# Grouped attention: one reciprocal for two units' row sums, and GpSimd scales both units' probabilities behind it

## What is computed

```
x = x + _layernorm(_L0_attn_ref(_layernorm(x)))
x = x + _layernorm(_L0_ffn_ref(_layernorm(x), factors, bias))
x = x + _layernorm(_L1_attn_ref(_layernorm(x), norm_scale, split_scale, Wq, Wk, Wv, Wo))
x = x + _layernorm(_L1_ffn_ref(_layernorm(x), gate_w, up_w, down_w, gate_s, up_s, down_s))
```

```
q = (h @ Wq.T).reshape(b, s, H, dh)      # H = 8 heads of dh = 64
k = (h @ Wk.T).reshape(b, s, G, dh)      # G = 2 groups, as v
scores = jnp.einsum('bghsd,bgtd->bghst', q, k) / np.float32(np.sqrt(dh))
attn = jax.nn.softmax(scores, axis=-1)
out = jnp.einsum('bghst,bgtd->bghsd', attn, v)
return x + out @ Wo.T
```

## Time and profile before

| | us |
|---|---|
| median of 3 runs | 1664.28 (1664.16 to 1665.33) |
| span of the profiled execution | 1664.7 |
| PE busy | 1499.3 (90%) |
| PEld busy | 1215.0 (73%) |
| DVE busy | 1049.3 (63%) |
| ACT busy | 789.7 (47%) |
| POOL busy | 733.6 (44%) |
| mean granted TensorE clock | 0.967 |

### The profile page before, as it was taken

How to read it: one execution, slowest core, us unless ns; L and a number is a source line. 1 busy time by engine, 2 the same in 40 slices (tenths; PEclk the granted TensorE clock), 3 DMA queues, 4 the chain that set the end, 5 groups by cost and what they waited for, 6 DMA issues and landing times.

```text
span 1664.7 us, 23612 instructions
## 1 busy us (share of the span) xinstructions
PE 1499.3 (90%) x7332; PEld 1215.0 (73%) x7332; DVE 1049.3 (63%) x2091; ACT 789.7 (47%) x1506; POOL 733.6 (44%) x914
## 2 busy tenths in 40 slices
PE   4999987986899998999899998679899999999996
PEld 3778766865678786878687876457688888888885
DVE  5688847875888887888788877545424234234233
ACT  2334335645877877787778776322212222222131
POOL 3476742653444544454445445313233333333331
PEclk9999997997999999999999999889999999999998
DMA  4122002232000202020202020232110110100100
GB/s 151 54 99 74 27 1 70 78 124 102 1 1 1 77 1 78 1 77 1 78 1 77 1 95 1 76 101 76 45 51 1 51 39 12 50 26 25 50 26 26
DMA packets 41814, 80.17 MB, mean 48 GB/s; under 512 B 2416, under 2 KB 3440, under 8 KB 41712
## 3 DMA queue, kind: packets, MB, share of 16 engines
q1 hardware_dynamic: 41712, 78.93, 14.0%
HBM read 53.75 MB, written 25.17 MB: 47 GB/s over the span
## 4 chain that ended last, share of the span: by engine, by line
PE 57%; DVE 9%; issue 4%; POOL 3%; ACT 3%; DMA 1%; POOLq 0%; DVEq 0%; SPq 0%; ACTq 0%
PE f_inner L57 22%; PE g_side L1375 12%; PE f_down L1786 9%; PE g_score L57 5%; PE g_turned L1395 5%; DVE g_ptl L1299 2%; PE g_output L1421 2%; PE g_output L1423 2%; DVE g_neg_max L1285 1%; DVE f_wl L1710 1%; PE f_inner L1758 1%; POOL g_power L984 1%; ACT g_pth L1161 1%; DVE g_q L1214 1%; DVE f_hidden L1679 1%
## 5 line engine op out<-in xcount | busy, mean ns | idle before, releaser
L1010 POOL TENSOR_SCALAR g_prob<-g_prob,g_inv_sum 128x512 f32<-128x512 f32 x256 | 178.7, 698 | 321.6 <-DVE g_inv_sum L1290 321.4
L57 PE MATMUL f_inner<-f_xth,f_wh 128*128 128x512 f32 x704 | 282.2, 401 | 16.2 <-DVE f_wl L1710 12.9
L57 PE MATMUL f_inner<-f_xtl,f_wh 128*128 128x512 f32 x704 | 280.7, 399 | 0.0
L1679 DVE SCALAR_TENSOR_TENSOR f_hidden<-f_inner,f_inner_scale,f_silu 128x512 f32<-128x512 f32 x88 | 66.0, 750 | 315.5 <-PE f_inner L57 315.5
L1568 POOL TENSOR_TENSOR f_hl<-f_hidden,f_hh 128x512 fp32r<-128x512 f32 x88 | 128.1, 1456 | 298.7 <-DVE f_hh L1685 298.7
L1620 ACT ACTIVATE f_silu<-f_inner,f_inner_scale 128x512 f32<-128x512 f32 x88 | 60.7, 690 | 415.8 <-PE f_inner L57 415.8
L1285 DVE TENSOR_REDUCE g_neg_max<-g_score 128x1 f32<-128x512 f32 x256 | 175.2, 685 | 94.9 <-PE g_score L57 93.8
L1119 ACT ACTIVATE g_prob<-g_score,g_neg_max 128x512 f32<-128x512 f32 x256 | 177.1, 692 | 96.5 <-DVE g_neg_max L1285 94.2
L1395 PE MATMUL g_turned<-identity,g_prob 128*128 128x128 f32 x1024 | 156.3, 275 | 37.2 <-DVE g_ptl L1299 24.6
L1299 DVE TENSOR_TENSOR g_ptl<-g_turned,g_pth 128x512 fp32r<-128x512 f32 x256 | 173.6, 678 | 16.4 <-ACT g_pth L1161 14.7
L1161 ACT CAST g_pth<-g_turned 128x512 fp32r<-128x512 f32 x256 | 149.5, 584 | 59.4 <-PE g_turned L1395 57.6
(11 more groups left out here) (200 smaller groups left out, 3456.8 us busy)
## 6 DMA issues: line engine op xcount, KB each, us to landing
x_resident<-x SPq DMA_DIRECT2D x8, 1024.0 KB, 7.3
x_mixed<-x_resident SPq DMA_DIRECT2D x8, 1024.0 KB, 4.3
x_pair<-x_mixed SPq DMA_DIRECT2D x8, 1024.0 KB, 7.5
g_res<-x_mixed SPq DMA_DIRECT2D x8, 1024.0 KB, 6.9
x_attended<-g_res SPq DMA_DIRECT2D x8, 1024.0 KB, 5.1
x_pair<-x_attended SPq DMA_DIRECT2D x8, 1024.0 KB, 5.5
factor<-factors SPq DMA_DIRECT2D x7, 1024.0 KB, 5.4
out<-x_pair SPq DMA_DIRECT2D x7, 1024.0 KB, 4.3
```

The costliest lines, as they stand in the source:

```text
L57: last = nc.tensor.matmul(out, lhsT, rhs, start=(n == 0), stop=(n == len(pairs) - 1))
L1010: nc.gpsimd.tensor_scalar(prob[:, at, :], prob[:, at, :], inv_sum[:, at:at + 1], 1.0, ALU.mult, ALU.mult).then_inc(prob_ready, 1)
```

## The change

The reciprocal is taken at even steps alone, of two neighbouring columns of `row_sum`, for units u-2 and u-1. POOL scales both units behind it at the even step, and nothing at the odd one. At an odd step the rest of POOL's and DVE's step stands where it did.

```diff
-            def normalise(g, u):
-                wait_alone(pool, s, inv_ready, g + 1)
-                at = u % 4
-                nc.gpsimd.tensor_scalar(prob[:, at, :], prob[:, at, :], inv_sum[:, at:at + 1],
-                                        1.0, ALU.mult, ALU.mult).then_inc(prob_ready, 1)
+            def normalise_pair(b, u):
+                wait_alone(pool, s, inv_ready, b * (UNITS // 2) + u // 2)
+                for at in ((u + 2) % 4, (u + 3) % 4):
+                    nc.gpsimd.tensor_scalar(prob[:, at, :], prob[:, at, :], inv_sum[:, at:at + 1],
+                                            1.0, ALU.mult, ALU.mult).then_inc(prob_ready, 1)
...
-                if u > 0 or not first:
+                if u % 2 == 0 and (u > 0 or not first):
                     if not drain or u == 0:
-                        normalise(b * UNITS + u - 1, u + 3)
+                        normalise_pair(b, u)
...
-                if (u > 0 or not first) and (not drain or u == 0):
-                    at = (u - 1) % 4
+                if u % 2 == 0 and (u > 0 or not first) and (not drain or u == 0):
+                    at = (u + 2) % 4
                     dve.wait_ge(exp_ready, g)
-                    nc.vector.reciprocal(inv_sum[:, at:at + 1], row_sum[:, at:at + 1]).then_inc(inv_ready, 1)
+                    nc.vector.reciprocal(inv_sum[:, at:at + 2], row_sum[:, at:at + 2]).then_inc(inv_ready, 1)
```

## The result

| | before | with the change |
|---|---|---|
| median, 5 runs each | 1665.33 us (1664.16 to 1666.41) | 1674.16 us (1670.60 to 1675.44) |
| ratio | | 1.0049, 95% interval 1.0035 to 1.0062 |
| span of the profiled execution | 1664.7 us | 1673.6 us |
| mean granted TensorE clock | 0.967 | 0.959 |

The change makes the kernel slower by 0.49%, some 8 us (the medians lie 8.8 us apart); 6.2 us (0.37%) had been forecast. The 1674.16 us stand just above the range's end of 1673.8; but the range was built on a median of 1664.28 before, and 1.0049 times that is 1672.4, inside it.

A forecast was written before the change was run, and what follows sets the result against it. It took TensorE (PE), busy 90% of the span, as the bound. 6 x (0.50 + 0.57 - 0.07) = 6.0, -0.2 for batch 0 and +0.4 for batch 7 gave +6.2 us: 1670.5 us (+0.37%), range 1665.2 to 1673.8.

The forecast's parts named there:

- PE's path: Steps 3 to 10: POOL's second scales part holds up ScalarE, then DVE, then PE's transposes; its delay forecast +0.50 us.
- Pair at step 4: POOL's second part of the next batch's scales starts behind two scalings, at 490.28 instead of 489.78: +0.50 us.
- Even unit: Unit 6's scaling now follows step 8's reciprocal, so PE's step 10 transposes come 1.17 behind it, not 0.86: +0.31 us.
- `g_ol` behind the pair: Step 8: POOL's `g_ol` queues behind two scalings, delaying PE's first output projection of step 10: +0.57 us, not given back.
- Odd reciprocals: Step 15's removed reciprocal shortens a gapless DVE row for which PE waits: -0.07 us; other odd steps then wait for PE.
- Batch 0: DVE-bound in steps 5 to 21: -0.07 in some six odd steps, +0.24 in one even step, -0.2 us.
- Batch 7: Same `g_ol` delay (+0.5), pairs +0.2 once or twice, odd steps 0.07 back three or four times: +0.4 us.
- Sum of the waits: Batches 1 to 6: 6 x (0.50 + 0.57 - 0.07) = 6.0 us, each batch 1.0 us longer.
- Rival (a): One of the two moves, `g_ol` or the second scales part, is absorbed: +3.0 us, 1667.3 us; chance 0.15.
- Rival (b): Slack of the even units and POOL's idle time leave only the small gains: 1664.3 us; chance 0.08.
- Rival (c): DVE's throughput is the bound, so 128 fewer reciprocals save 9.0 us: 1655.3 us; chance 0.06.
- Rival (d): DVE's cast to `g_oh` at step 0 is held through both scalings: 1.2 us on top, 1671.7 us; chance 0.07.

The follow-up runs named there:

- e3: The change, but at step 4 the second part of the next batch's scales stands ahead of POOL's pair of scalings; ratio 0.9996 to the kernel before.
- e7: The kernel before, without pairs, with two small operations on POOL ahead of the second part of the scales, about 0.56 us later; ratio 1.0039.
- e8: The kernel before, without pairs, with four small operations on POOL ahead of the second part of the scales, 1.12 us later; ratio 1.0069.
- e9: The kernel before, without pairs, with both parts of the scales ahead of the scaling at steps 3 and 4; ratio 0.9989.
- e4: The change with the second part of the scales ahead of step 4's pair and `g_ol` between step 8's two scalings; ratio 1.0001 to the kernel before.
- e2: The change, but at step 8 `g_ol` stands between the two scalings; ratio 1.0048 to the kernel before.
- e1: The change's one reciprocal for two units, but POOL scales one unit a step; ratio 0.9990 to the kernel before.
- e5: The change, but each even step has two reciprocals of one column instead of one of two; ratio 1.0052 to the kernel before.
- e10: The change's pairing, reciprocal and both scalings, moved to the odd steps; ratio 0.9991 to the kernel before.

## Why the prediction was right, and where it fell short

- *PE's path runs through POOL's part 1, ScalarE's gapless row and DVE's.* Right, each link late by 0.50 us, as forecast; e3, e7 and e8 show it, and e9 how far it goes the other way.
- *Pair at step 4, +0.50 for part 1.* Measured 0.51.
- *Even unit, +0.31 at step 10.* Measured 0.24: PE followed `g_prob`'s end (500.48 + 0.69 = 501.17) within 0.05 us, not 0.12.
- *`g_ol` behind the pair, +0.57 including the 0.31.* The load came 0.58 later (1.08 less the 0.50), but what stayed was less: batch 1's later steps are 0.93 late, not 1.08. That PE "isn't given back" anything was wrong by 0.15; e4 against e3 prices the queue at 0.22 us, not 0.26.
- *Odd reciprocals, -0.07 at step 15.* Measured 0.06. *Batch 0, -0.2:* measured -0.4. *Batch 7, +0.4:* without its two half-clock stretches it can't be read; with them +1.4. Here PE waits for `g_prob` at the even steps 8, 16, 24, 28 and 30 too, which the prediction had named, for even steps other than 10, as a sign of being wrong; in batches 1 to 6 it does so at none.
- *Sum of the waits:* 0.87 us a batch against the 1.0 forecast, 5.2 against 6.0 us. That the whole change still came out near the forecast is in part luck: the clock added 4.8 us that the sum had not, and the smaller waits, the branches (1.0) and a half-clock stretch less in the last stage (1.7) made up for a part.
- *The step that failed* is the one that ends the sum, that a batch costs its waits and nothing else. The clock was read as 1.00 in batch 1 and taken as 1.00 for the rest. Nor do the batches have the same step lengths, as the prediction says: before the change they were 80.32, 85.35, 81.81, 85.50, 81.79 and 80.40 us long, with the branches at the ends of 2 and 4 and half clock at the starts of 3 and 5. With the longer standstills came half-clock stretches of 3.4 us in five of six batches (2.7 us), and the loop's own stretch caught more work (2.1 us): 4.8 of the 9.1 us that batches 1 to 6 lost, against 1.0 that came back at the branches. Without all that the change would have been near 0.3%, as its one run at a clock of 0.967 was.
- *Rival (a), one of the two moves absorbed:* neither was. Part 1 came through in full, and the queue of `g_ol` with 0.17 (e2) to 0.22 us (e4 against e3) of the 0.26. *Rival (b), nothing to be seen:* refuted by the result. *Rival (c), DVE's throughput:* e1 and e5 refute it; 128 fewer reciprocals bought nothing that runs can tell.
- *Rival (d), the cast held through both scalings:* refuted by the profile. DVE and POOL at step 0 of batch 1 after the change, against the earlier trace rows:

```profile
478.48 0.67 DVE L1251 CAST g_oh<-g_out_sum 128x512 fp32r<-128x512 f32 x1
```

```profile
478.18 1.52 POOL L1010 TENSOR_SCALAR g_prob<-g_prob,g_inv_sum 128x512 f32<-128x512 f32 x2 [3.60 <-DVE g_inv_sum L1290]
```

The cast takes 0.67 as before. It is the second scaling that waits: the pair takes 1.52 here and 1.37 elsewhere. The stage has 17 such second scalings, of 0.85 to 0.87 us each, and no cast behind a pair is longer than 0.69.

## What to carry to other kernels

An engine that is idle half of the time can still be on the path, through one small operation behind a bulky one: before two bulky instructions are put together, look at what stands behind them in that engine's queue and who waits for it. Shifting the pairs by one step, or putting the small operation first, made the difference of 0.5%; batching itself saved nothing that the timed runs can tell (0.9991 for e10), since the instructions saved were hardly on the path. And where TensorE stands still more, price the clock as well, and over several repetitions, since one repetition may be spared.

## What the hardware showed that was not expected

A DVE cast between two SBUF tensors that meets a running GpSimd instruction seems to be let in between it and the next one of a back-to-back pair: in the 17 places the cast takes 0.56 to 0.69 us, as behind one scaling before, and the second GpSimd instruction takes 0.85 instead of 0.70 (the longest of L1010, 865 ns, against 818 before). The granted clock fell to 1.2 GHz behind several standstills in a row, each of about 1 us or less (in batch 7 one of 2.4 us is among them), at the same place of batches 3 to 7 in two profiles, yet in batch 2 in only one of them.
